# Preparing the feed-forward weights and row statistics one program earlier, and splitting a decoder's weights in sixteenths

## What is computed

```python
x = x + _L0_xattn_ref(ctx_1024, _layernorm(x, axis=-1), L0_xattn_ln1_g, ...)   # 16 heads of 64 over context and latents
x = x + _L0_attn_ref(_layernorm(x, axis=-1), L0_attn_Wq, ...)                   # linear attention, relu(q), relu(k)
x = x + _L0_ffn_ref(_layernorm(x, axis=-1), L0_ffn_w_gate, L0_ffn_w_up, L0_ffn_w_down)
x = x + _L1_xattn_ref(_layernorm(x, axis=-1), ctx_1024, ctx_1024, mask, ...)    # masked cross attention, 16 heads of 16
x = x + _L1_attn_ref(_layernorm(x, axis=-1), L1_attn_ln_w, ...)                 # a gated recurrence over 64 rows
x = x + _L1_ffn_ref(_layernorm(x, axis=-1), L1_ffn_Wr, ...)                     # 8 experts, gates by 25 bisections
```

## Time and profile before

| | |
|---|---|
| median of 3 runs | 2268.39 us (2262.28 to 2269.05) |
| the profiled execution | 2264.27 us, its span 2262.6 us |
| PE busy | 2148.3 us (95% of the span) |
| DVE, ACT, POOL busy | 1196.1, 1078.7, 527.5 us |
| mean granted clock of PE | 0.976 of full |
| `latent_attention` ends, `linear_feed` starts | 911.9, 913.2 us |
| `linear_feed` ends, `decoder` starts | 1139.9, 1141.1 us |
| a `bn_stats` of one tile | 412 ns |
| loads issued at the start of `linear_feed` | 11, 3.5 MB |

### The profile page before, as it was taken

How to read it: one execution, slowest core, us unless ns; L and a number is a source line. 1 busy time by engine, 2 the same in 40 slices (tenths; PEclk the granted TensorE clock), 3 DMA queues, 4 the chain that set the end, 5 groups by cost and what they waited for, 6 DMA issues and landing times. The chain is left out here.

```text
span 2262.6 us, 51163 instructions
## 1 busy us (share of the span) xinstructions
PE 2148.3 (95%) x21377; PEld 1880.7 (83%) x21377; DVE 1196.1 (53%) x3542; ACT 1078.7 (48%) x2427; POOL 527.5 (23%) x411
## 2 busy tenths in 40 slices
PE   6999999999999999589869999999999999999999
PEld 6888888898989888357748888878988889998898
DVE  5655555555555554566546678842867432323311
ACT  4545454545454454233227676653444344444444
POOL 1000000000000000432211212233454454445544
PEclk9999999999999999699989999999999999999999
DMA  4001000000000000200031101010101001011000
GB/s 140 20 16 29 17 19 20 16 20 15 20 16 20 16 6 1 66 1 1 1 103 31 32 30 31 12 39 1 57 1 38 23 16 38 1 38 38 1 10 29
DMA packets 48804, 58.12 MB, mean 26 GB/s; under 512 B 6528, under 2 KB 40128, under 8 KB 48448
## 3 DMA queue, kind: packets, MB, share of 16 engines
q1 hardware_dynamic: 48576, 54.85, 7.7%
HBM read 46.72 MB, written 2.10 MB: 22 GB/s over the span
## 5 line engine op out<-in xcount | busy, mean ns | idle before, releaser
L846 POOL TENSOR_TENSOR moe_h<-moe_hr,moe_h 128x512 fp32r<-128x512 f32 x256 | 358.6, 1401 | 427.9 <-ACT moe_hr L1158 427.9
L1157 ACT ACTIVATE moe_h<-bank,dec_b 128x512 fp32r<-128x512 f32 x256 | 176.3, 689 | 416.0 <-PE bank L83 412.9
L2141 DVE TENSOR_REDUCE lat_neg_max<-bank 128x1 f32<-128x320 f32 x256 | 113.7, 486 | 319.8 <-PE bank L1922 319.8
L83 PE MATMUL bank<-lat_wv,lat_kv_t 128*128 128x256 f32 (+1 forms) x1728 | 265.8, 304 | 10.3 <-ACT lat_v L2016 3.9
L83 PE MATMUL bank<-lat_kv_t,lat_wk 128*128 128x320 f32 x1536 | 256.3, 316 | 0.0
L83 PEld LDWEIGHTS bank<-lat_wv,lat_kv_t 128*128 128x128 f32 x1728 | 224.9, 191 | 33.8 <-ACT lat_v L2016 5.7
L83 PEld LDWEIGHTS bank<-lat_kv_t,lat_wk 128*128 128x128 f32 x1536 | 225.8, 188 | 0.1
L1512 DVE SCALAR_TENSOR_TENSOR x_sb<-bank,moe_xs,x_sb 128x256 f32<-128x256 f32 x96 | 39.8, 477 | 349.2 <-PE bank L1015 349.1
L83 PE MATMUL bank<-dec_xt,dec_lo 128*128 128x512 f32 x512 | 202.3, 395 | 0.0
L1618 POOL TENSOR_TENSOR lat_rs_rstdc<-lat_rs_varc,lat_rs_halfc 128x4 f32<-128x4 f32 x16 | 16.2, 1014 | 767.3 <-DVE lat_rs_varc L1610 767.3
L2030 ACT ACTIVATE lat_p<-bank,lat_neg_max 128x320 f32<-128x320 f32 x256 | 137.0, 535 | 114.0 <-DVE lat_neg_max L2141 114.0
(11 more groups left out here) (318 smaller groups left out, 4031.8 us busy)
## 6 DMA issues: line engine op xcount, KB each, us to landing
raw_w<-in_L_ffn_W SPq DMA_DIRECT2D x16, 1024.0 KB, 6.9
lat_ctx_raw<-in_ctx SPq DMA_DIRECT2D x16, 512.0 KB, 4.1
att_ctx_raw<-in_ctx_turned SPq DMA_DIRECT2D x16, 512.0 KB, 3.7
lat_kv_t<-lat_lt SPq DMA_DIRECT2D x32, 128.0 KB, 2.2
out_x<-x_sb SPq DMA_DIRECT2D x4, 512.0 KB, 2.9
x_sb<-in_x SPq DMA_DIRECT2D x1, 1792.0 KB, 14.9
lat_xl_now<-lat_xl SPq DMA_DIRECT2D x7, 256.0 KB, 4.5
lat_raw<-in_L_xattn_Wq SPq DMA_DIRECT2D x1, 1024.0 KB, 7.4
```

The costliest lines, as they stand in the source:

```text
L83: mm = pe.matmul(out, lhs(a, k), rhs(b, k), start=first and k == 0 and n == 0, stop=last and k == KD - 1 and n == 2)
L846: pool.tensor_tensor(h[:, g % 2, 1, :], hr[:, g % 2, :], h[:, g % 2, 0, :].bitcast(F32), ALU.subtract).then_inc(h_lo, 1)
L1157: act.activation(h[:, n % 2, 0, :], h_bank[n % 2][:, :], ACT.Relu, bias=bias).then_inc(h_hi, 1)
L2141: dve.tensor_reduce(neg_max[:, u:u + 1], s_bank[h][:, 0:LK], AX.X, ALU.max, negate=True).then_inc(s_max, 1)
```

## The change

A new object, `Ahead`, lives over the first two programs. It holds one room of 128 x 4608, the linear attention's weights `wq`, `wkv` and `bq`, and the statistics `norm` and `shift` of `linear_feed`. `latent_attention` uses the room for its `raw0` and `raw1`. After its second couple of pairs SP loads the integer weights into the room and the linear attention's weights beside them; at the sixth context POOL turns the integers to floats in place, in nine pieces. In pairs 1 to 12 DVE adds one `bn_stats` per pair (slot 4) of the tile that is final by then, and every fourth pair a `close` (slot 5); POOL makes power and shift. So the statistics of chunks 0 to 2 are ready when `linear_feed` starts; those of chunk 3 are made where they were.

`linear_feed` loads only biases, gamma and beta. All splitting of its feed-forward weights is on DVE now, at the start, in six operations. In `decoder`, the query weights are loaded first and have a count of their own, the key and value weights another. The context's split stands ahead of DVE's weight halves and of POOL's fourth power, the mask's operation behind. Expert 2's weights are split in 16 pieces of 128 x 512, one in each of bisections 8 to 23; those of experts 3 to 7 in pieces before single operations of `weigh`, in the first three chunks of the expert before. `weigh_first` is cut in four: chunk c of experts 0 and 1 is added behind chunk c of expert 2. The diff, cut to its core:

```diff
@@ class Ahead (new)
+    def __init__(self, nc, ctx):
+        self.wq, self.wkv = tools.sb("wq", [P, KD, D]), tools.sb("wkv", [P, KD, 2 * D])
+        self.bq = tools.sb("bq", [P, KD])
+        self.room = tools.sb("room", [P, 3 * KD * self.HID])
+        self.norm = TileStats(tools, None, None, "ahead", minus=True)
+        self.shift = tools.sb("shift", [P, NT])
...
+    def power_and_shift(self, pool, ready, c):
+        norm, at = self.norm, slice(c * NT // NCH, (c + 1) * NT // NCH)
+        norm.power(pool, c)
+        pool.wait_ge(norm.rstd_ready, c - norm.first + 1)
+        pool.tensor_tensor(self.shift[:, at], norm.mean[:, at], norm.rstd[:, at], ALU.mult).then_inc(ready, 1)
@@ latent_attention, SP
+            def load_ahead():
+                sp.wait_ge(w_lo[1], 1)
+                sp.wait_ge(w_lo[3], 1)
+                for g, n in enumerate(("gate", "up")):
+                    sp.dma_start(k.ahead.weights_up()[:, :, g, :].bitcast(I32), rows(w["L0_ffn_w_" + n])).then_inc(ahead_in, 16)
+                sp.dma_start(k.ahead.weights_down().bitcast(I32), rows(w["L0_ffn_w_down"])).then_inc(ahead_in, 16)
+                sp.dma_start(k.ahead.wq[:, :, :], rows(w["L0_attn_Wq"])).then_inc(ahead_whole, 16)
...
             for c in range(COUPLES):
                 couple(c, last=c == COUPLES - 1)
+                if c == 1:
+                    load_ahead()
@@ latent_attention, POOL
             for i in range(2, NT):
                 norm_c.power(pool, i * norm_c.steps)
+                if i == 6:
+                    pool.wait_ge(ahead_in, 48)
+                    for n in range(9):
+                        piece = k.ahead.room[:, n * CH:(n + 1) * CH]
+                        pool.tensor_scalar(piece, piece.bitcast(I32), 1.0 / 127.0, None, ALU.mult)
+                if i % 4 == 1 and i // 4 <= Ahead.CHUNKS:
+                    k.ahead.power_and_shift(pool, ahead_shift, i // 4 - 1)
@@ latent_attention, DVE slot
+                if s == 4 and 1 <= i <= 4 * Ahead.CHUNKS:
+                    dve.wait_ge(x_done, i)
+                    k.ahead.norm.row(dve, x_sb[:, i - 1, :], i - 1)
+                if s == 5 and 1 <= i <= 4 * Ahead.CHUNKS and i % 4 == 0:
+                    k.ahead.norm.close(dve, i // 4 - 1)
@@ linear_feed, SP
-            sp.dma_start(wq[:, :, :], rows(w["L0_attn_Wq"])).then_inc(loads, 16)
-            sp.dma_start(wkv[:, :, 0:D], rows(w["L0_attn_Wk"])).then_inc(loads, 16)
-            sp.dma_start(wkv[:, :, D:2 * D], rows(w["L0_attn_Wv"])).then_inc(loads, 16)
...
-            sp.dma_start(wi[:, :, 0, :], rows(w["L0_ffn_w_gate"])).then_inc(ffn_loads, 16)
-            sp.dma_start(wi[:, :, 1, :], rows(w["L0_ffn_w_up"])).then_inc(ffn_loads, 16)
-            sp.dma_start(wdi[:, :, :], rows(w["L0_ffn_w_down"])).then_inc(ffn_loads, 16)
-            sp.wait_ge(loads, 128)
...
+            sp.wait_ge(loads, 64)
@@ linear_feed, POOL
-            power_and_shift(norm_l, shift_l, l_shift, 0)
-            pool.wait_ge(ffn_loads, 48)
-            pool.tensor_scalar(wf[:, :], wi[:, :], 1.0 / 127.0, None, ALU.mult).then_inc(gu_float, 1)
-            pool.wait_ge(loads, 128)
+            pool.wait_ge(loads, 64)
             add_beta(0)
-            pool.tensor_scalar(wdf[:, :], wdi[:, :], 1.0 / 127.0, None, ALU.mult).then_inc(wd_float, 1)
-            low_weights_up()
-            power_and_shift(norm_l, shift_l, l_shift, 1)
             norm_y.power(pool, 0)
...
-            low_weights_down()
@@ linear_feed, PE and ACT
             turn_rows(0)
-            pe.wait_ge(loads, 128)
             queries(0)
...
             def rows_apply(c):
-                act.wait_ge(l_shift, c + 1)
+                if c == Ahead.CHUNKS:
+                    act.wait_ge(l_shift, 1)
...
-            act.wait_ge(loads, 128)
             queries(0)
...
-                    if c == 0 and i == 0:
-                        act.wait_ge(gu_float, 1)
-                        act.copy(wgu[:, 0], wf[:, :]).then_inc(gu_hi, 1)
@@ linear_feed, DVE
-            rows_stats(0)
-            norm_l.close(dve, 0)
-            dve.wait_ge(loads, 128)
-            dve.wait_ge(consts, 5)
+            for kd in range(KD):
+                dve.tensor_copy(wgu[:, 0, kd], wf[:, kd]).then_inc(gu_hi, 1)
+            dve.tensor_copy(wd[:, 0], wdf).then_inc(wd_hi, 1)
+            for kd in range(KD):
+                dve.wait_ge(gu_hi, kd + 1)
+                dve.tensor_tensor(wgu[:, 1, kd], wf[:, kd], wgu[:, 0, kd].bitcast(F32), ALU.subtract).then_inc(gu_lo, 1)
+            dve.wait_ge(wd_hi, 1)
+            dve.tensor_tensor(wd[:, 1], wdf, wd[:, 0].bitcast(F32), ALU.subtract).then_inc(wd_lo, 1)
+            dve.wait_ge(loads, 64)
...
-                    if i == 0 and c + 1 < NCH:
+                    if i == 0 and c + 1 == Ahead.CHUNKS:
                         rows_stats(c + 1)
@@ decoder, SP
+            sp.dma_start(wq[:, :, :], rows(w["L1_xattn_Wq"])).then_inc(q_loads, 16)
...
+            sp.dma_start(wkr, rows(w["L1_xattn_Wk"])).then_inc(kv_loads, 16)
             context(0)
+            sp.dma_start(wvr, rows(w["L1_xattn_Wv"])).then_inc(kv_loads, 16)
@@ decoder, POOL
-            for c in range(NCH):
+            for c in range(NCH - 1):
                 norm_a.power(pool, c)
             split_keys(0)
+            norm_a.power(pool, NCH - 1)
@@ decoder, PE, ACT and DVE
-            pe.wait_ge(loads, 16 * 11)
+            pe.wait_ge(q_loads, 32)
             queries(0)
...
-            act.wait_ge(loads, 16 * 11)
+            act.wait_ge(kv_loads, 48)
...
-            dve.wait_ge(loads, 16 * 11)
+            dve.wait_ge(q_loads, 32)
...
-            s.give(dve.tensor_scalar(mask[:, :], mask_i, 0.0, MASKED, ALU.is_equal, ALU.mult))
+            split_keys(0)
             dve.wait_ge(w_hi, 2)
@@ decoder, DVE, experts
+            def split_piece(e, n):
+                par, which, low_part, at = e % 2, n // 8, n % 8 >= 4, slice(n % 4 * F // 2, (n % 4 + 1) * F // 2)
+                if n == 0:
+                    dve.wait_ge(w_in[par], 32 * (e // 2) + 32)
+                if not low_part:
+                    dve.tensor_copy(hi[par][:, which, at], raw[par][:, which, at]).then_inc(e_high, 1)
+                    return
+                dve.wait_ge(e_high, 8 * (e - 2) + 4 * which + n % 4 + 1)
...
                 for it in range(BISECTIONS):
                     step = 0.5 ** (it + 1)
+                    if 8 <= it < 24:
+                        split_piece(2, it - 8)
...
-            split_weights(2)
-            weigh_first()
+            dve.wait_ge(gates_ready, 1)
...
             for e in range(2, E):
-                add_output(e, 0)
-                add_output(e, 1)
-                if e + 1 < E:
-                    split_weights(e + 1)
-                add_output(e, 2)
-                add_output(e, 3)
+                for c in range(NCH):
+                    add_output(e, c, e + 1 < E and c < 3)
+                    if e == 2:
+                        weigh_first(c)
```

145 lines of the change are left out of this document (83 added, 62 removed).

## The result

The changed kernel took **2226.09 us** (median of 4 runs, 2222.97 to 2227.17), the kernel before 2265.34 (median of 4, 2261.53 to 2269.05). The ratio is 0.9828, 95% interval 0.9814 to 0.9842. The profiled executions took 2264.27 and 2225.31 us, spans 2262.6 and 2223.3.

What follows compares the result with a forecast made beforehand. PE bounds the latent attention; gains lie in the later programs' starts and an experts' hole. 5.8 + 10.9 + 6.5 + 8.5 + 3.3 - 1.0 = 34.0 us off 2264.27 gives 2230.3, plus 1.7: 2232 (2227 to 2237; wider 2221 to 2244).

Steps and rivals of the forecast that it cites:

- Part 1: Start of `linear_feed`: with statistics and weights made ready by the program before, `queries` starts earlier; 5.8 us won.
- rival 1: Second program starts no faster than DVE or clock lets it; gives back 5 to 8 us, 2239; chance 0.14.
- Part 2: Holes between `linear_feed`'s tile steps: each step falls to 3.60 us without POOL's holds and queued statistics; 10.9 us won.
- bound of 6.4: Lower bound for Part 2's gain in us: if PE's clock stays low, each step may stay about 1.5 us longer.
- Part 3: Latent attention pays for added DVE statistics and nine POOL multiplications, mostly hidden; cost 1.0 us, upper bound for statistics 7.8.
- 2.5 us of idle per slot: Latent attention: DVE's 2.50 us idle before a slot's first reduction was to absorb 0 to 4 us of holds by POOL.
- The sign in the table of stages: Table of program lengths: `latent_attention` was forecast at +1.0 us; the measured difference was -1.4.
- Part 4: Decoder's start: reordered loads and an earlier context split remove PE's waits; 6.5 us won, bounds 3 and 8.24.
- Part 5: Hole in the experts: weighing experts 0 and 1 chunk by chunk removes the 6.14 us stall and its clock; 8.5 us.
- Rival 4: Hole in the experts only moves: DVE falls behind at expert 2's third chunk, PE waits there; 2236; chance 0.08.
- Part 6: Experts' weights split in sixteenths no longer hold POOL's step, so PE waits less; 3.3 us won, upper bound 3.6.
- Rival 5: More is won: the clock stays up through the starts and both decoder waits go whole; 2224; chance 0.13.

Runs made afterwards that it cites:

- x10: Changed kernel, but `linear_feed`'s low feed-forward weight parts are made on POOL, the 128 x 3072 subtraction only behind the second tile's keys; 2236.45 us.
- x6: Changed kernel, but all statistics of the second program's first normalisation are made in that program again, the first chunk's ahead of DVE's weight halves; 2233.76 us.
- x9: Changed kernel, but PE makes the router's products one tile a step, 6 matmuls at a time over 16 steps; 2218.19 us, ratio to before 0.9803.

## Why the forecast was right, and where it was not

| part | forecast | measured in the trace |
|---|---|---|
| 1 start of `linear_feed` | 5.8 | 5.8 at `queries`, 4.8 at the first `kpre` |
| 2 holes between tiles | 10.9 | 10.9 |
| 3 latent attention pays | -1.0 | -1.6 (and +3.0 of clock) |
| 4 decoder's start | 6.5 | 7.9 |
| 5 hole in the experts | 8.5 | 9.6 with part 6's share in that stretch |
| 6 sixteenths | 3.3 | 6.5 over the other stretches; 9.1 when undone (8.0 by the medians) |
| not forecast | | -3.0, expert 0's clock (-1.6 where it fell once) |

**Part 1**: the working held, down to `queries` 4.8 us behind the first instruction. It needed both halves of the move, which I had not said. 1 us went to a slower `queries`. DVE had 3.4 us to spare, not 2.1 (1.0 of it because `queries` was slower), and rival 1 came only in that 1 us of clock.

**Part 2**: steps of 3.60 us, as said (21.68 us from first to fourth `kpre` before, 10.80 after). The cause was named right for the long sum; the removal of the subtraction from POOL was not needed, only that it no longer met a sum of two SBUF tiles. The collision alone made a step of 8.74 us again (x10); the statistics alone cost 0.9 us (x6). The bound of 6.4 was too careful about the clock.

**Part 3**: a cost, as said, in the place of the multiplications. "2.5 us of idle per slot" failed as an argument, since nine in a row hold DVE through two slots: its four normalisations (L1655) took 2.37 us, 1.37 before. These are `tensor_scalar` operations with one tile as input:

```profile
330.23 1.37 DVE L1621 TENSOR_SCALAR lat_ctx_n<-lat_ctx_raw,lat_rs_meanc,lat_rs_rstdc 128x256 f32<-128x256 f32 x4
```

The Trainium skill (SBUF — State Buffer, "Who interferes with whom") says that `tensor_scalar` can enter a two-port mode, if its operands allow it, and can then contend with GpSimd; the trace agrees for these four and for two of L2212 (0.72 and 0.82 us), though one of L2212 beside the same POOL work, at 326.31, took its usual 0.39. In the prediction I counted only sums of two tiles, and had a row against that in the trace of before. There I took the multiplication as not holding DVE to its end, since one sum was over at 943.50; but the `tensor_scalar` just behind it lasted until 944.39, with POOL's end at 944.37:

```profile
943.69 0.70 DVE L118 TENSOR_SCALAR body_ts_meanl<-body_ts_tmpl 128x4 f32<-128x4 f32 x1
```

The statistics in the other slots cost nothing that shows. The sign in the table of stages is the clock's.

**Part 4**: 1.4 us above my value and inside its bounds; the next bound was DVE, as said.

**Part 5**: the stall and its clock went, 9.2 us if expert 2's stretch is set against the 89.35 that an undisturbed one took before. Rival 4 did not come: PE has no wait on DVE there.

**Part 6** is the term that was mis-sized, 3.3 against 6.5. I priced it by the idle time of the matmul rows in one view. The stretches between two loads were in the trace of before and give the true price: 91.57 against 90.03.

**The sum.** 34.0 us were forecast between the profiled executions, 39.3 came by their spans. Of the 5.3 between, 2.4 are in the latent attention (3.0 of clock less 0.6), 0.3 in `linear_feed`, 2.6 in `decoder` (parts 4 to 6 together 5.6 more, expert 0's clock 3.0 less). The two clock terms were not in the sum, and that they cancel (3.0 each) is luck. Rival 5 (more is won) had the size nearly right and its cause in half: `decoder` won 7.9 of the 8.24 us of its two waits, but the clock did not stay up through the start of `linear_feed` (`queries` 6.75 us).

## What to carry to other kernels

Price contention by the distance of two fixed points in the program, one stretch with it and one without, and not by the idle time of one kind of row. Before you move work off GpSimd, look which VectorE operations run beside it: with one operand in PSUM they were not held at all, with two in SBUF for its whole length, so another moment may do as well as another engine. Where two chains end at the same start, shortening one buys only the distance to the other.

## What the hardware showed that I had not expected

- TensorE's clock fell to 1.2 GHz with the engine busy 10.00 of 10.00 us, inside or just behind a group of 24 matmuls of 8 columns, in all twelve traces that have such groups. In groups of six over 16 steps the clock stayed at 2.4 GHz (two traces), and expert 0 took 6.4 to 7.9 us less. A busy share of 100% is no sign of full clock; the granted clock has to be read.
- Not only DVE is held: POOL's power on four columns took 1.63 us beside DVE's casts in place of 1.02, its shift 0.81 in place of 0.24 (x6).
- A hole of 5.30 us in PE cost a further 2.4 us in the step behind it (6.02 in place of 3.60).
- Over the traces of the changed kernel and its variants the first program ends between 908.8 and 914.0 us; its granted clock over 17 to 36 us was 0.82, 0.91 or 1.00 in them. The runs of one kernel lie 0.6 us (x6) to 7.7 us (x9) apart; with one trace of each it is not shown how much of that this clock makes.
